# First sparse layer: logits three tiles ahead, attention rows on GpSimd, query jobs in front of the logits and behind the turning

## The reference

```
score = softmax(gelu(batchnorm(grouped_conv(z))) @ lin_w.T + lin_b)   # once for "out", once for "in"
s_v, s_i = top_k(score, 32)                                            # of 256, per token
out_branch = scatter(take(z @ W, s_i_out) * s_v_out)
in_branch  = scatter(take(z, s_i_in) * s_v_in) @ W
y = out_branch + in_branch + bias
```

## Time and profile before

| | |
|---|---|
| median of 3 runs | 1379.68 us (1375.58 to 1380.49) |
| profiled execution: time, span | 1381.49 us, 1379.8 us |
| busy PE / DVE / ACT / POOL | 1218.1 / 1149.0 / 1054.9 / 963.6 us |
| chain that ended last, by engine | PE 57%, DVE 13%, issue 13%, ACT 12%, POOL 4% |
| mean granted clock of TensorE | 0.968 |

### The profile page before, as it was taken

How to read it: one execution, slowest core, us unless ns; L and a number is a source line. 1 busy time by engine, 2 the same in 40 slices (tenths; PEclk the granted TensorE clock), 3 DMA queues, 4 the chain that set the end, 5 groups by cost and what they waited for, 6 DMA issues and landing times.

```text
span 1379.8 us, 30641 instructions
## 1 busy us (share of the span) xinstructions
PE 1218.1 (88%) x10192; PEld 743.8 (54%) x10192; DVE 1149.0 (83%) x3141; ACT 1054.9 (76%) x2350; POOL 963.6 (70%) x1094
## 2 busy tenths in 40 slices
PE   3999999767888879999999999999999999667776
PEld 1455554334455536665666666666666666344444
DVE  6999998479998888888777787878777854799998
ACT  3432333677899869999999989999999985777775
POOL 4457644368777767778777778777777773488887
PEclk9999999989999999999999999999999999899997
DMA  6200000000012000000000000000000000000000
GB/s 174 77 1 1 0 1 0 1 1 1 12 36 77 31 17 25 25 25 25 25 13 14 2 2 2 2 3 2 2 2 2 2 2 1 1 31 17 31 17 31
DMA packets 35529, 25.32 MB, mean 18 GB/s; under 512 B 16358, under 2 KB 32044, under 8 KB 35372
## 3 DMA queue, kind: packets, MB, share of 16 engines
q1 hardware_dynamic: 35372, 23.36, 6.0%
HBM read 14.89 MB, written 8.39 MB: 17 GB/s over the span
## 4 chain that ended last, share of the span: by engine, by line
PE 57%; DVE 13%; issue 13%; ACT 12%; POOL 4%; DVEq 0%; DMA 0%; SPq 0%; ACTq 0%; POOLq 0%
PE banks L1978 7%; PE banks L1980 6%; PE banks L1966 6%; DVE arena L1492 4%; PE banks L1716 4%; PE banks L1924 4%; PE banks L1995 4%; PE banks L1996 4%; PE banks L1997 3%; DVE arena L1487 3%; ACT arena L1140 3%; PE banks L1675 3%; ACT arena L1148 2%; PE banks L1731 2%; PE banks L1900 2%
## 5 line engine op out<-in xcount | busy, mean ns | idle before, releaser
L819 POOL TENSOR_TENSOR arena<-arena 128x512 f16<-128x512 f32 x383 | 438.0, 1163 | 150.1 <-ACT arena L1148 146.4
L1140 ACT ACTIVATE arena<-banks 128x512 f32<-128x512 f32 x512 | 303.1, 600 | 45.1 <-PE banks L1980 40.3
L1566 DVE TENSOR_REDUCE arena<-banks 128x1 f32<-128x512 f32 x512 | 325.5, 679 | 5.1 <-PE banks L1966 2.8
L1148 ACT ACTIVATE arena<-arena 128x512 f16<-128x512 f32 x512 | 315.9, 632 | 0.0
L1487 DVE MAX8 arena<-arena 128x8 f32<-128x256 f32 x512 | 190.6, 414 | 27.4 <-issue 15.9
L1995 PE MATMUL banks<-arena 128*128 128x65 f16 x2016 | 211.3, 193 | 1.1
L1996 PE MATMUL banks<-arena 128*128 128x64 f16 x2016 | 211.4, 195 | 0.0
L1997 PE MATMUL banks<-arena 128*128 128x65 f16 x2016 | 210.5, 192 | 0.0
L1592 DVE TENSOR_TENSOR arena<-arena 128x512 f16<-128x512 f32 x129 | 106.8, 828 | 123.6 <-ACT arena L1148 123.5
L1492 DVE MATCH_REPLACE8 arena<-arena 128x256 f32<-128x256 f32 x512 | 206.0, 410 | 0.4 <-issue 0.2
L1995 PEld LDWEIGHTS banks<-arena 128*128 128x128 f16 x2016 | 187.9, 96 | 32.0 <-issue 10.1
(11 more groups left out here) (223 smaller groups left out, 2543.3 us busy)
## 6 DMA issues: line engine op xcount, KB each, us to landing
arena<-q_store SPq DMA_DIRECT2D x48, 128.0 KB, 2.7
x<-in_L_attn_a_x SPq DMA_DIRECT2D x8, 512.0 KB, 3.9
q_store<-arena SPq DMA_DIRECT2D x32, 128.0 KB, 1.8
out<-x SPq DMA_DIRECT2D x7, 512.0 KB, 2.9
arena<-arena SPq DMA_DIRECT2D x64, 1.0 KB, 1.9
arena<-in_L_attn_a_W_in SPq DMA_DIRECT2D x1, 768.0 KB, 5.7
arena<-in_L_attn_a_W_mid SPq DMA_DIRECT2D x1, 512.0 KB, 7.5
arena<-in_L_attn_a_w_w SPq DMA_DIRECT2D x2, 256.0 KB, 7.8
```

Source lines behind the costliest of these rows:

```text
L819: nc.gpsimd.tensor_tensor(pr_lo[c][:, kt, :], pr[:, kt, :], pr_hi[c][:, kt, :], ALU.subtract).then_inc(a_lP, 1)
L1140: nc.scalar.activation(pr[:, kt, :], ps[6 + kt % 2][:, :], ACT.Exp, scale=SM_SCALE).then_inc(a_P, 1)
L1148: nc.scalar.activation(pr_hi[c][:, kt, :], pr[:, kt, :], ACT.Copy).then_inc(a_hi, 1)
L1566: nc.vector.tensor_reduce(mx_half[c][:, i // 2, i % 2:i % 2 + 1], ps[n % MAX_BANKS][:, :], X, ALU.max).then_inc(a_mx, 1)
```

## The change

- `lg` gets three buffers (`LG_RING`). ScalarE's copy of the logits and TensorE's product run three tiles ahead instead of two, in both sparse layers; logits(2) are made right after full(0), and copied within the GELU loop after chunk 5.
- The rows z of the attention move from ScalarE (`attn_row` in `head_second`) to GpSimd (`head_rows`, behind `tail` and `rstd_of`), and the table gives them one step earlier.
- TensorE, step t: full(t), turning z(t+2), jobs of HEAD_AT[t], logits(t+3), (t = 31: first maxima), `ffn_in`(t), corrections of HEAD_AT[t].
- ScalarE, step t: z(t+2), rest(t), zT(t+2), exp(t+1), sT(t), fs(t), copies of HEAD_AT[t], logits(t+3), gs(t), low copies of HEAD_AT[t].

```diff
+LG_RING = 3
-        lg = [carve([2, D]) for _ in range(2)]
+        lg = [carve([2, D]) for _ in range(LG_RING)]
-        HEAD_ROWS_AT = {8: (0, 1), 9: (2, 3), 12: (4,), 13: (5,), 14: (6, 7), 16: (8,), ...
+        HEAD_ROWS_AT = {7: (0, 1), 8: (2, 3), 11: (4,), 12: (5,), 13: (6, 7), 15: (8,), ...
@@ GpSimd, ffn(f), per tile
+                    if f == 0:
+                        head_rows(t)
+            def head_rows(t):
+                for r in HEAD_ROWS_AT.get(t, ()):
+                    k, j = r // TPC, r % TPC
+                    if j == 0:
+                        pool.wait_ge(n_p, 4 * group_of["ffn", k] + 4)
+                        pool.wait_ge(s_tps, 2 * (LN_ATTN + max(0, k - 1)) if k != 1 else 2 * LN_ATTN)
+                    last = nc.gpsimd.tensor_scalar(z_rows[k % 2][:, j, :], x[:, r, :], rs[:, r, 0:1], rs[:, r, 1:2],
+                                                   ALU.mult, ALU.add)
+                    if j == TPC - 1:
+                        last.then_inc(s_z, 1)
@@ ScalarE, ffn(f)
-                    if n in (1, 3):
-                        ffn_logits(f, n // 2, n // 2)
+                    if n in (1, 3, 5):
+                        ffn_logits(f, n // 2, 0)
                     ffn_rest(f, t, q)
-                    if f == 0:
-                        head_first(t)
                     ffn_zT(f, t + 2, q)
                     ffn_exp(f, t + 1, 1 - q)
                     ffn_sT(f, t, q)
                     ffn_fs(f, t, q)
-                    ffn_logits(f, t + 2, q)
+                    if f == 0:
+                        head_first(t)
+                    if t + 3 < NT:
+                        ffn_logits(f, t + 3, 1 - q)
+                    ffn_gs(f, t, q)
                     if f == 0:
                         head_second(t)
-                    ffn_gs(f, t, q)
@@ ScalarE and TensorE: head_first, head_second
-                for what, k, part, bank in HEAD_AT.get(t - 1, ()):
+                for what, k, part, bank in HEAD_AT.get(t, ()):
@@ TensorE, ffn(f)
                     ffn_full(f, t, t % 2)
+                    if t == 0:
+                        ffn_logits(f, 2, 0)
                     if t + 2 < NT:
-                        ffn_front(f, t + 2, t % 2)
+                        ffn_z_turned(f, t + 2, t % 2)
+                    if f == 0:
+                        head_first(t)
+                    if t + 3 < NT:
+                        ffn_logits(f, t + 3, 1 - t % 2)
+                    if f == 0 and t == NT - 1:
+                        first_maxima()
+                    ffn_in(f, t, t % 2)
                     if f == 0:
                         head_second(t)
-                    ffn_in(f, t, t % 2)
-                    if f == 0:
-                        head_first(t)
```

More of the change, by code:

```diff
@@ L376, in hybrid_block_kernel @@
         HEAD_STATS_AT = {6: 0, 10: 1, 14: 2, 18: 3}
-        HEAD_ROWS_AT = {8: (0, 1), 9: (2, 3), 12: (4,), 13: (5,), 14: (6, 7), 16: (8,), 17: (9,), 18: (10,), 19: (11,),
-                        21: (12,), 22: (13,), 23: (14,), 24: (15,)}
+        HEAD_ROWS_AT = {7: (0, 1), 8: (2, 3), 11: (4,), 12: (5,), 13: (6, 7), 15: (8,), 16: (9,), 17: (10,), 18: (11,),
+                        20: (12,), 21: (13,), 22: (14,), 23: (15,)}
         HEAD_AT = {
@@ L988, in ffn_logits @@
                 act.wait_ge(f_lps, T + 1)
-                nc.scalar.activation(lg[p], ps[1][:, :].rearrange("p (k c) -> p k c", k=2),
+                nc.scalar.activation(lg[t % LG_RING], ps[1][:, :].rearrange("p (k c) -> p k c", k=2),
                                      ACT.Copy).then_inc(f_lg, 1)
@@ L1001, in ffn_exp @@
                 for i in range(2):
-                    nc.scalar.activation(ex[p][:, i, :], lg[p][:, i, :], ACT.Exp, bias=nm[p][:, i:i + 1],
+                    nc.scalar.activation(ex[p][:, i, :], lg[t % LG_RING][:, i, :], ACT.Exp, bias=nm[p][:, i:i + 1],
                                          accum_out=sm[p][:, i:i + 1]).then_inc(f_e, 1)
@@ L1183, in head_second @@
                                              ACT.Copy).then_inc(h_qlo, 1)
-                for r in HEAD_ROWS_AT.get(t, ()):
-                    attn_row(r // (2 * TPC), r % (2 * TPC))
             ffn(0)
@@ L1482, in topk_round @@
                 for i in range(2):
-                    src = lg[p][:, i, :] if r == 0 else wk[p][:, i, (r - 1) % 2, :]
+                    src = lg[t % LG_RING][:, i, :] if r == 0 else wk[p][:, i, (r - 1) % 2, :]
                     if r:
@@ L1800, in _ @@
             over_chunks(pe, lru_step)
-            def ffn_front(f, t, p):
-                ffn_z_turned(f, t, p)
-                ffn_logits(f, t, p)
             def ffn_z_turned(f, t, p):
@@ L2054, in head_second, with first_maxima @@
                            start=False, stop=True, skip_group_check=True).then_inc(h_qmps, 1)
[L2055 to L2061, removed]
+            def first_maxima():
+                pe.wait_ge(f_lg, NT)
+                for i in range(2):
+                    max_scores(0, i)
+                pe.wait_ge(*head_read[2])
+                for i in range(2, HALVES):
+                    max_scores(0, i)
             ffn(0)
```

## The result

The changed kernel takes 1392.06 us (median of 4, 1391.01 to 1392.82) against 1379.25 (median of 4, 1375.58 to 1380.49): ratio 1.0091, 95% interval 1.0075 to 1.0107. It is slower by 12.8 us; 8.8 was forecast, or 1388.5 us. (A fourth run of the kernel before moved its median from 1379.68 to 1379.25.) The profiled execution took 1392.8 us with a span of 1390.9, 11.1 more than the span before.

The account below looks back on a forecast made before the run. The prediction took TensorE and ScalarE, waiting on each other beside attention work in the first sparse layer, as the bound. Rows +1.6, the 17 steps +8.1 and the end -0.9 gave +8.8, or 1388.5 us; range 1375 to 1395.

Parts of the forecast that it names:

- What bounds: First sparse layer with attention work: TensorE and ScalarE set the pace together; VectorE's stalls are what they leave over.
- The 14 us: VectorE's top-k waits for logits in the first sparse layer, 14.0 us: the most that deeper logits can bring.
- The query step: First sparse layer, in-product to in-product with a query job: 6.63 us against 6.39, TensorE waiting 0.6 for z.
- the ring: First sparse layer, TensorE and ScalarE waiting on each other; 17 steps to tile 28 take 125.5 us against 117.4, +8.1.
- Surcharges: Extra time in the 17 steps for turnings, keys, latents and the second query, with their ScalarE copies: 12.8 us.
- Rows on GpSimd: Attention rows given to GpSimd lengthen steps before tile 11 of the first sparse layer: +1.6 us, bounds 0 and 2.5.
- Start of the layers: Both sparse layers: the wait saved before tile 2 is offset by a later first exp: 0, bounds -1.5 and +1 each.
- End: First sparse layer, in-product of tile 28 to first maxima, step 29 without query: 13.4 us against 14.4, -0.9.
- The sum: Whole kernel: +1.6 + 8.1 - 0.9 = +8.8 us, or 1388.5 us on the median.
- TensorE finds z ready: Rival: z comes within 2.06 us of the in-product, steps run at TensorE's own 6.02; about 1369 us, chance 0.20.
- The surcharges hide: Rival: ScalarE's head copies fall into unseen waits in the 17 steps; 1380.7 us, no change, chance 0.22.
- The lower clock: Rival: short waits bring 1.2 GHz back, two or three spells of 1.6 us more; 1392 to 1395 us, chance 0.10.

Follow-up runs that it names:

- the logits alone: Kernel before with three logits buffers and logits made three tiles ahead, all else as before: 1381.09 us, ratio 1.0002.
- one more copy: Changed kernel with an unused 128x256 ScalarE copy before z(t+2) in steps 12 to 28 of the first sparse layer: 1395.9 us, ratio 1.0126.
- both moves alone: Changed kernel with z(t+3) made right behind exp(t+1) and ScalarE's head copies put before sT(t): 1376.3 us, ratio 0.9966 to the kernel before.

## Why the prediction was right, and where its terms were off

**What bounds.** Right, and tested from both sides. Three logits alone took away some 5 us of VectorE's waits for nothing, and one ScalarE instruction moved in TensorE's favour gave about 10 us. The 14 us were left over by the ring.

**The query step.** 6.63 us forecast, 6.60 measured; its point, the turning at 2.67 behind the in-product, was met to the hundredth (408.88 to 411.55). TensorE's own 6.02 was measured as 5.99 once z came early. One row was misread on the way: the wait of 0.69 us at 345.10 does not show the ring. Two attention rows stand in ScalarE's queue in front of gs there, and z starts half a microsecond later for it:

```profile
343.10 1.09 ACT L1096 ACTIVATE zrow<-x,rs 128x256 f32<-128x256 f32 x2
344.08 0.48 ACT L1016 ACTIVATE arena<-banks,arena 128x256 f32<-128x256 f32 x1
344.44 0.61 ACT L972 ACTIVATE arena<-x,rs 128x256 f32<-128x256 f32 x1
```

Without such rows the turning's wait for z in the kernel before is 0.19 us (steps to tiles 1 to 5). The forecast did not rest on this row.

**Surcharges.** Forecast steps and measured ones: with turnings 7.50 and 7.48; behind them 7.61 and 7.58 (tiles 20, 25; 7.71 at tile 15); behind a latent 7.17 and 7.09; behind a keys job, with a latent of its own, 7.37 and 7.55; behind keys alone (tile 21) 7.17 and 7.32; with the second query 9.0 and 8.81; behind it 7.63 and 7.57. The 17 steps: 125.5 forecast, 126.0 measured; step 19 alone makes this difference, and the other misses, none above 0.2 us, cancel. The keys term is 0.15 too small, and in that slot the instruction behind the 64-partition low copy starts 0.6 us later, not 0.49 (last section). Step 19 was the one that was not merely mis-sized: "one row hides there, and an rstd just about" took each by itself, but table and statistics put both in step 18, and it cost 0.6 more than 7.50.

**Rows on GpSimd.** In steps 8 to 11, 6.55, 6.55, 6.64 and 7.4 forecast, 6.74, 6.91, 6.60 and 7.55 measured. Which share of it is GpSimd's is not separated: with the rows back on ScalarE the four steps take 27.6 us together, with them on GpSimd 27.8; in the old order the rows alone make them 26.5 instead of 25.5. Relative to the layer's start the delay at tile 11 was 1.4 us, the term +1.6; this is in part luck. From tile 7 on, where the term counts, it was 2.3 us, and 0.9 had been gained before, which the next paragraph takes for scatter.

**Start of the layers.** 0 forecast. The reciprocal of tile 0 waits 1.58 us in the run with the logits alone, as forecast, and 0.54 in the changed kernel; the 1.44 us in front of tile 2 are gone in both. The first layer's in-product of tile 7 lies 54.5 us behind the first MAX8 in the changed kernel and 55.4 before, but over the twelve traces anywhere from 54.2 to 56.7, so nothing is told here in either direction. From the first MAX8 of the second layer to the end of the span it is 198.3 before and 198.4 after: 0 there.

**End.** -0.9 forecast, 0.0 measured: this is the term that failed. From the in-product of tile 28 to the first maxima it is 14.37 us in both. Steps 29 and 30 took 5.74 and 5.59 where 5.45 was forecast for each, and 3.04 us followed behind the last in-product where the earlier trace rows had 2.55: +0.29, +0.14 and +0.49, which eats the 0.9. Some 0.6 of it is the clock. TensorE idled for 2.56 us before the last turning; from this turning to the in-product it took 1.04 us instead of 0.88, and the in-product took 2.08 us instead of 1.13. The 0.29 of step 29 is not; there TensorE waits 1.74 us for the sparse rows.

```profile
496.24 0.41 PE L1853 MATMUL banks<-ident,arena 128*128 128x128 f32 x2 [1.74 <-POOL arena L748]
497.13 1.13 PE L1857 MATMUL banks<-fW,arena 128*128 128x256 f32 x4 [0.47 <-ACT arena L1043]
498.09 1.03 PE L1844 MATMUL banks<-fW,arena 128*128 128x256 f32 x4
501.68 0.56 PE L1853 MATMUL banks<-ident,arena 128*128 128x128 f32 x2 [2.56 <-POOL arena L748]
502.72 2.08 PE L1857 MATMUL banks<-fW,arena 128*128 128x256 f32 x4 [0.47 <-ACT arena L1043]
```

Three stretches of it, columns as in the first fence:

```profile
495.00:499.00 4.00, 2.28 (x10) 1.64 (x10) 4.00 (x18) 2.71 (x10) 3.73 (x6) 1.00 0.07 23
499.00:502.40 3.40, 0.68 (x3) 0.20 (x2) 2.06 (x10) 1.87 (x8) 3.12 (x6) 0.91 0.00 0
502.40:505.00 2.60, 2.28 (x5) 1.85 (x6) 0.00 (x0) 0.80 (x3) 1.95 (x3) 0.50 0.00 0
```

The granted clock is 1.00, the 2.4 GHz level, around the wait of 1.74 us, and 0.50, which is 1.2 GHz, behind that of 2.56 us. In the kernel before, the same idle time stood there and the clock fell too, only later: its in-product (491.73) still took 1.13 us, the full product behind it 1.79, at 0.52 over 492.7:495.

```profile
490.85 0.41 PE L1843 MATMUL banks<-ident,arena 128*128 128x128 f32 x2 [2.56 <-POOL arena L747]
...
492.70 1.79 PE L1834 MATMUL banks<-fW,arena 128*128 128x256 f32 x4
```

So the 2.55 us taken from the earlier trace rows held a part of the lower clock. In the kernel with the logits alone a wait of 2.55 us was followed by no fall, and from the in-product to the first maxima it took 1.83 us (490.80 to 492.63). So its end took 13.61 us in the old order. In the changed order the kernel with one more copy had its low clock earlier and 1.83 us at the same place, and its end took 13.32. Like laid beside like, the order shortens the end by 0.3 us and not by 0.9; in this execution the clock took that away too.

```profile
490.00:493.00 3.00, 2.53 (x12) 1.87 (x13) 0.00 (x0) 1.77 (x5) 2.60 (x5) 1.00 0.00 0
```

**The sum.** +8.8 forecast. The trace has +9.6 from the layer's start on: 1.4 + 8.6 + 0.0 - 0.4. The medians have +12.8, with an interval of 10.3 to 14.8 by the ratio, and the 9.6 lies below it. Some 1.2 us of the gap are the step to tile 12 of the trace before, which ran in part at the lower clock: against a ring without it the trace has +10.8. Whether the other executions of the kernel before are free of it is not shown. The prediction had priced this spell at 1.6 us and still left it in the 117.4 that it subtracted, while its 125.5 is built of steps without one; so +8.1 is too small for the ring by this much. That it lies so near to the measured 8.6 comes in part from both being reckoned against the same 117.4. The last 2 us stay open.

**The rivals.** "TensorE finds z ready" was refuted for the change and then made true by hand: 1369 had been worked out for it, 1374.5 to 1376.3 came. With both moves alone, the 17 steps take 3.3 us more than its 107.3 (1.1 of it step 19), the steps up to tile 11 1.8 more than it counted, and the end some 1.5. "The surcharges hide" was refuted by the step behind turnings, 7.58. The lower clock did not return in the ring of the changed kernel: the granted clock was 1.00 over 370:480 again, with 0.93 us of waits in each query step instead of 0.68. The rule of the Trainium skill ("TensorE: Matmul & The Clock Gate", What's actually happening), that activity releases the throttle, agrees with the stretch 502.4:505, at 0.50 behind the two long waits. The waits of half a microsecond in the ring did not bring it on, and neither did the 2.55 us in the kernel with the logits alone.

## What to carry to other kernels

A step that two in-order queues hand to and fro is as long as the chain through both; before an instruction is moved, write down that chain with pitches, starting from the last result that each queue waits for, and see what stands in front of the operand that the other engine will want first. Work goes where a queue waits anyway, which here was behind the exponentials and in front of sT(t), and not behind a result that comes late. Idle time of an engine that only follows, VectorE's 14 us here, is neither a price nor a gain: it can be removed for nothing, and comes back under another name.

## What the runs showed of the hardware

In these traces the next instruction of ScalarE starts before the row of the one before it ends. From start to start it is 0.49 for rows of 0.60 (128x512 copies and 128x256 with a scale and bias from memory), 0.37 for 0.48, 0.32 for 0.42; but 0.62 from the 64-partition low copy of the keys to the row behind it (399.36 to 399.98 in the kernel with rows on ScalarE). Another copy of 64 partitions, with the logits' copy behind it, took 0.48 (397.91 to 398.39); why the two differ is not shown. A normalised row of 128x256 took GpSimd 0.55 us beside VectorE's top-k, as it had in front of the second sparse layer, where no top-k runs. A wait of TensorE of 2.56 us was followed by the lower clock in the changed kernel and in the one before, and one of 2.55 us was not in the kernel with the logits alone; what decides is not shown.
